# A graph network kernel: destination terms of two convolutions in SBUF by blocks of 128 rows, in place of a DMA per tile

## The reference

```python
def mesh_conv(x, src, dst, ea, w1, b1, g, bt, w2, b2):
    m = jnp.concatenate([x[dst], x[src], ea], axis=-1) @ w1 + b1
    m = jax.nn.silu(group_norm(m, g, bt))
    m = m @ w2 + b2
    out = jax.ops.segment_sum(m, dst, num_segments=n)
    ...
```

## Time and profile before

| what | value |
|---|---|
| median of 3 runs | 13,936.2 us (13,921.76 to 13,947.93) |
| span of the profiled execution | 13,635.3 us |
| its own time | not given apart from the span |
| instructions | 222,101 |
| PE matmul busy | 8536.7 us (63%) |
| DVE busy | 6628.8 us (49%) |
| POOL busy | 6588.0 us (48%) |
| ACT busy | 4239.7 us (31%) |
| convolution gathers, line 548 | 3232, 3299.7 us, mean 1021 ns |
| window matmuls, line 570 | 6464 MATMULs, 990.1 us |
| window DMAs, line 534 | 3232 of 64.0 KB |

### The profile page before, as it was taken

The page is one execution under the profiler, slowest core; times in us unless marked ns, Lnnn a source line. Parts: engine busy times, 40 slices in busy tenths (PEclk is TensorE's granted clock), DMA queues, the critical chain, the costliest instruction groups (busy, mean ns, idle before and its releaser), DMA issues. The chain is left out here.

```text
span 13635.3 us, 222101 instructions
## 1 busy us (share of the span) xinstructions
PE 8536.7 (63%) x44314; PEld 6779.2 (50%) x44314; DVE 6628.8 (49%) x13722; ACT 4239.7 (31%) x19386; POOL 6588.0 (48%) x6618
## 2 busy tenths in 40 slices
PE   3666666656566666666455556556547777777775
PEld 2444444444344444444344445445436676766664
DVE  4555555556555555555644444444453333333335
ACT  1333333333233333333222222222213333333332
POOL 4555555553455555555255555555314444444441
PEclk7777777777677777777677777777757777787776
DMA  3333333332333333333344444444334343334333
GB/s 105 87 87 89 88 88 88 88 88 69 88 87 88 87 88 89 88 87 89 90 130 130 130 131 130 129 128 129 108 77 90 88 91 89 89 89 90 88 89 88
DMA packets 1712372, 1319.86 MB, mean 97 GB/s; under 512 B 623557, under 2 KB 1489166, under 8 KB 1711480
## 3 DMA queue, kind: packets, MB, share of 16 engines
q1 hardware_dynamic: 1471910, 772.17, 20.8%
q0 software_dynamic: 237088, 539.87, 15.4%
q10 hardware_dynamic: 2610, 1.32, 0.0%
HBM read 1252.35 MB, written 60.09 MB: 96 GB/s over the span
## 5 line engine op out<-in xcount | busy, mean ns | idle before, releaser
L548 POOL DMA_INDIRECT conv_gath<-b,conv_idx x3232 | 3299.7, 1021 | 3065.9 <-DMA conv_n<-in_n_b 2120.8
L584 PE MATMUL conv_sums<-conv_hot,conv_m 128*128 128x128 f32 x6464 | 1407.6, 367 | 2188.9 <-ACT conv_m L637 1705.6
L908 POOL DMA_INDIRECT gat_gath<-g,gat_idx x1616 | 1577.6, 976 | 1956.8 <-DVE gat_val L1154 1224.5
L584 PEld LDWEIGHTS conv_sums<-conv_hot,conv_m 128*128 128x128 f32 x6464 | 1215.5, 266 | 2572.1 <-ACT acc L625 1358.5
L908 POOL DMA_INDIRECT attn_gath<-kv,attn_idx x1616 | 1583.3, 980 | 1619.0 <-DVE attn_val L1154 938.5
L672 DVE TENSOR_REDUCE conv_var<-conv_sq 128x32 f32<-128x512 f32 x808 | 550.0, 681 | 2661.3 <-ACT conv_sq L614 2335.0
L623 ACT ACTIVATE acc<-conv_sums,acc 128x1 f32 x3232 | 844.6, 261 | 2489.9 <-remote 1866.1
L570 PEld LDWEIGHTS conv_z<-conv_win,conv_hotT 128*128 128x128 f32 x6464 | 992.2, 217 | 650.4 <-issue 650.4
L939 PE MATMUL gat_p_edge<-weta,gat_xeT 128*128 128x136 f32 x3232 | 891.1, 369 | 367.8 <-ACT gat_edge L1010 280.4
L1030 ACT COPY small<-attn_smalls 40x127 f32 x1616 | 417.3, 258 | 2221.4 <-remote 1310.0
L570 PE MATMUL conv_z<-conv_win,conv_hotT 128*128 128x128 f32 x6464 | 990.1, 299 | 147.9 <-issue 134.2
(11 more groups left out here) (356 smaller groups left out, 16331.1 us busy)
## 6 DMA issues: line engine op xcount, KB each, us to landing
conv_win<-a SPq DMA_DIRECT2D x3232, 64.0 KB
conv_places<-places SPq DMA_DIRECT2D x202, 512.0 KB
attn_win<-q SPq DMA_DIRECT2D x1616, 64.0 KB
gat_xeT<-in_xeT SPq DMA_DIRECT2D x404, 256.0 KB
conv_gath<-b,conv_idx POOLq DMA_INDIRECT x3232
attn_places<-places SPq DMA_DIRECT2D x101, 512.0 KB
gat_places<-places SPq DMA_DIRECT2D x404, 128.0 KB
attn_gath<-kv,attn_idx POOLq DMA_INDIRECT x1616
```

The costliest lines, as they stand in the source:

```text
L548: pool.indirect_dma_start(gath[:, b.c * BQ + k, t, :], None, b_table, bass.IndirectOffsetOnAxis(ap=idx[:, b.c, k * QT + t:k * QT + t + 1], ...
L584: mm = nc.tensor.matmul(sums[so][:, t * P:(t + 1) * P], m[:, k, t * P:(t + 1) * P], hot[:, k, t, :], start=True, stop=True)
L908: pool.indirect_dma_start(gath[:, b.c * BQ + k, t, :], None, table, bass.IndirectOffsetOnAxis(ap=idx[:, b.c, k * QT + t:k * QT + t + 1], a ...
```

## The change

The a terms never go to DRAM. The node stage's ACT copies them into an SBUF tensor `table` of 49 blocks of 128 rows plus one block of zeros: row r of block k is in partition r. A tile's destinations span less than 128 nodes from its first one on, so they lie in the block of the first node or the next. For each tile PE multiplies two one-hots (offsets from the block's start against the partition number, and against that plus 128) with two blocks of `table`, whose address comes from a PE register. The places per tile are replaced by offsets, and a new small DMA brings 16 block bases with the metadata. The starts' DMA, SP's register load, the window DMAs and their buffers are gone. PE's step is the same order of quads and sums, cut at another point, with one load of 16 registers at the head of each batch's quads.

```diff
+            link(nc.vector.tensor_scalar(base_q[:, :], n0_q[:, :], 7, 7, ALU.logical_shift_right, ALU.logical_shift_left))
+            link(nc.vector.tensor_tensor(off_q[:, :].rearrange("q (t e) -> q t e", e=P),
+                                         dst_q[:, :].rearrange("q (t e) -> q t e", e=P),
+                                         bc(base_q[:, :].unsqueeze(2), [P, TQ, P]), ALU.subtract))
...
-            def fetch(b, nxt, _):
-                if nxt:
-                    fetch_starts(nxt)
+            def fetch(b, *_):
...
-                                 (places[:, b.c, :], places_of(D, b.i * EB, EB)),
+                                 (places[:, b.c, :], offsets_of(D, b.i * EB, EB)),
...
+                                 (bases_in[:, b.c, :], D["bases"][:, bass.ds(b.i * TB, TB)]),
...
-                _, starts = nc.values_load_multi_w_load_instructions(
-                    starts_in[0:1, b.c, :], engines=(SP_ENGINE,), min_val=0, max_val=N,
...
-                for k in range(BQ):
-                    done(sp, z_ready, b.quad(k) - WQ + 1)
-                    settle(sp, st.passed)
-                    for t in range(QT):
-                        sp.dma_start(win[:, k, t, :], a_table[bass.ds(starts[k * QT + t], P), :])\
-                          .then_inc(win_landed[k], 16)
...
+            def blocks(b):
+                pe.wait_ge(meta_landed[b.c], (b.q + 1) * META)
+                settle(pe, st.passed)
+                _, bases = nc.values_load_multi_w_load_instructions(
+                    bases_in[0:1, b.c, :], engines=(PE_ENGINE,), min_val=0, max_val=(NBLK - 1) * P,
...
-                pe.wait_ge(win_landed[s4], (b.i + 1) * QT * 16)
                 done(pe, hotT_ready, b.quad(k) + 1)
                 for t in range(QT):
-                    nc.tensor.matmul(zb[:, t * P:(t + 1) * P], hotT[:, s6, t * P:(t + 1) * P], win[:, s4, t, :],
-                                     start=False, stop=False, skip_group_check=True)
+                    for half in range(2):
+                        nc.tensor.matmul(zb[:, t * P:(t + 1) * P], hotT[:, s6, half, t * P:(t + 1) * P],
+                                         a_cols[:, bass.ds(bases[k * QT + t] + half * P, P)],
+                                         start=False, stop=False, skip_group_check=True)
...
+                if after:
+                    bases = blocks(after)
+                    pre_activation(after, 0, bases)
+                sum_up(b, 1)
+                sum_up(b, 2)
+                sum_up(b, 3)
+                if after:
+                    pre_activation(after, 1, bases)
+                    pre_activation(after, 2, bases)
+                    pre_activation(after, 3, bases)
+                if nxt:
+                    sum_up(nxt, 0)
...
-                nc.vector.tensor_scalar(hotT[:, s6, :], places[:, b.c, k * QE:(k + 1) * QE], C["iota_col"][:, 0:1], None, ALU.is_equal)\
+                nc.vector.tensor_scalar(hotT[:, s6, 0, :], places[:, b.c, k * QE:(k + 1) * QE], C["iota_col"][:, 0:1], None, ALU.is_equal)
+                nc.vector.tensor_scalar(hotT[:, s6, 1, :], places[:, b.c, k * QE:(k + 1) * QE], C["iota_col"][:, 1:2], None, ALU.is_equal)\
                   .then_inc(hotT_ready, 1)
...
-                    act.copy(made[:, :, 0:2 * P], pwb).then_inc(evacuated, 1)
+                    act.copy(table[:, bass.ds(g * GB, GB), :], pwb[:, :, 0:P])
+                    act.copy(made[:, :, 0:P], pwb[:, :, P:2 * P]).then_inc(evacuated, 1)
```

More of the change, by code:

```diff
@@ L187, in sem, with prepare @@
         return s
-def prepare(nc, w, C, D, R):
+def prepare(nc, w, C, D, R, table):
     with Stage(nc, "prep") as st:
@@ L492, in conv_edges @@
         gath_landed = [st.sem(f"gath_landed{n}") for n in range(GQ)]
-        win_landed = [st.sem(f"win_landed{n}") for n in range(WQ)]
-        starts_landed = [st.sem(f"starts_landed{c}") for c in range(RB)]
         hotT_ready, hot_ready, var_ready, normed, u_ready = (
@@ L558, in _, with pre_activation @@
             pe.wait_ge(zeroed, 2)
-            def pre_activation(b, k):
-                s6, s4, s12 = (b.c * BQ + k) % PQ, k, b.c * BQ + k
+            def blocks(b):
[3 more added lines that the diff above has]
+                    bases_in[0:1, b.c, :], engines=(PE_ENGINE,), min_val=0, max_val=(NBLK - 1) * P,
+                    skip_runtime_bounds_check_because="first nodes of blocks that hold destinations")
+                return bases
+            def pre_activation(b, k, bases):
+                s6, s12 = (b.c * BQ + k) % PQ, b.c * BQ + k
                 zb = z[s12 % ZQ]
-                pe.wait_ge(meta_landed[b.c], (b.q + 1) * META)
                 done(pe, normed, b.quad(k) - ZQ + 1)
@@ L599, in step @@
                 sum_up(b, 3)
-            for k in range(BQ):
-                pre_activation(Batch(0, 0), k)
-            pre_activation(Batch(0, 1), 0)
+                if after:
[4 more added lines that the diff above has]
+                    sum_up(nxt, 0)
+            for b in (Batch(0, 0), Batch(0, 1)):
+                bases = blocks(b)
+                for k in range(BQ):
+                    pre_activation(b, k, bases)
+            sum_up(Batch(0, 0), 0)
             run_batches(pe, step)
@@ L1314, in blocks_of, with node_stage @@
     return table[bass.ds(g * GW, GW), :].rearrange("(b p) c -> p b c", p=P)
-def node_stage(nc, kind, w, C, D, cnt, acc, acc_e, small, out, R=None):
+def node_stage(nc, kind, w, C, D, cnt, acc, acc_e, small, out, R=None, table=None):
     soft = kind in ("attn", "gat")
@@ L1363, in node_stage @@
         LOADS = 16 * {"first": 1, "conv1": 0, "conv2": 1, "attn": 3, "gat": 3}[kind]
-        STORES = 16 * {"first": 3, "conv1": 2, "conv2": 3, "attn": 4, "gat": 1}[kind]
+        STORES = 16 * {"first": 2, "conv1": 1, "conv2": 3, "attn": 4, "gat": 1}[kind]
         wide = [P, GB, P]
@@ L1823, in build @@
         cnt = sb("cnt", [P, 2, NBLK])
-        with ExitStack() as ranks:
-            def kept(name, shape, dt=F32):
-                return ranks.enter_context(nc.sbuf_tensor(f"rank_{name}", shape, dt))
-            R = {"node": kept("node", [P, NBLK]), "below": kept("below", [P, NBLK, P]),
-                 "n0_rows": kept("n0_rows", [P, NBLK, TB], I32), "dst_rows": kept("dst_rows", [P, NBLK, P], I32),
-                 "batch": kept("batch", [P, NBLK]), "batch_i": kept("batch_i", [P, NBLK], I32),
-                 "tile": kept("tile", [P, 2, NBLK + 1]), "tile_i": kept("tile_i", [P, NBLK], I32),
-                 "degree": kept("degree", [P, NBLK]), "shift": kept("shift", [P, P]), "corner": kept("corner", [P, P])}
-            prepare(nc, w, C, D, R)
-            node_stage(nc, "first", w, C, D, cnt, None, None, None, out, R)
@@ L1836, in build, with kept @@
-        with nc.sbuf_tensor("acc1", [P, NW], F32) as acc:
-            conv_edges(nc, 1, w, C, D, acc)
-            node_stage(nc, "conv1", w, C, D, cnt, acc, None, None, out)
-            conv_edges(nc, 2, w, C, D, acc)
-            node_stage(nc, "conv2", w, C, D, cnt, acc, None, None, out)
+        with nc.sbuf_tensor("table", [P, NBLK + 1, P], F32) as table:
+            with ExitStack() as ranks:
+                def kept(name, shape, dt=F32):
+                    return ranks.enter_context(nc.sbuf_tensor(f"rank_{name}", shape, dt))
+                R = {"node": kept("node", [P, NBLK]), "below": kept("below", [P, NBLK, P]),
+                     "n0_rows": kept("n0_rows", [P, NBLK, TB], I32), "dst_rows": kept("dst_rows", [P, NBLK, P], I32),
+                     "batch": kept("batch", [P, NBLK]), "batch_i": kept("batch_i", [P, NBLK], I32),
+                     "tile": kept("tile", [P, 2, NBLK + 1]), "tile_i": kept("tile_i", [P, NBLK], I32),
+                     "degree": kept("degree", [P, NBLK]), "shift": kept("shift", [P, P]), "corner": kept("corner", [P, P])}
+                prepare(nc, w, C, D, R, table)
+                node_stage(nc, "first", w, C, D, cnt, None, None, None, out, R, table)
+            with nc.sbuf_tensor("acc1", [P, NW], F32) as acc:
+                conv_edges(nc, 1, w, C, D, acc, table)
+                node_stage(nc, "conv1", w, C, D, cnt, acc, None, None, out, None, table)
+                conv_edges(nc, 2, w, C, D, acc, table)
+                node_stage(nc, "conv2", w, C, D, cnt, acc, None, None, out)
```

54 lines of the change are left out of this document (27 added, 27 removed).

## The result

| | time, us | ratio to before |
|---|---|---|
| before, median of 4 | 13,940.28 (13,921.76 to 13,947.93) | |
| after, median of 4 | 14,106.94 (14,058.73 to 14,150.32) | 1.0116 (1.0087 to 1.0144) |
| forecast | 13,235 (12,300 to 14,600) | |

The forecast had the wrong side: 167 us slower, 0.83 us for each of the 202 batches, where 707 us faster was expected. The time lies inside the range only because the range reached over to the rivals on that side. The profile of after has a span of 14,104.0 us, within 3 us of that execution's own time (14,105.77), while the one of before lies 305 us under the median of its runs. So the two profiles alone would overstate the change.

A forecast was written before the change was run, and what follows sets the result against it. No engine fills the period; a loop of waits bounds it. A batch of 21.5 + 2.5 + 3.1 = 27.1 us for 30.6 saves 707 us over 202 batches; 13,936.2 less 707 plus 6 is 13,235 us (12,300 to 14,600).

The forecast's parts named there:

- (f): In the gathers' burst: without window DMAs the stall starts only when SP issues metadata; period 27.1 us for 30.6.
- the stall: In the later half of a burst of gathers, ACT stands still for 11.76 us and SP issues DMAs slowly.
- (c): PE's 32 more MATMULs and weight loads a batch: 4.2 to 7.0 us, covered unless PE is caught in the stall.
- (a): Window DMAs, starts' load and register load leave SP's queue: 1.05 us a batch saved on average, half eaten by bases DMA.
- (b): DVE's second one-hot per quad: 2.0 us a batch, added whole, so the working stretch goes from 18.4 to 20.4 us.
- (d): PE loads 16 registers and forms 32 addresses a batch: 2.4 us at most, 0 if its sequencer runs ahead.
- PE is caught in the stall: In the convolutions, part of PE's matmuls falls behind the stall: period 33.65 us, time 14,558 us; chance 0.25.
- The variant of the first rival: In the convolutions, DVE's one-hots hold up POOL's gathers: burst 2.0 us longer, 404 us in all, time 13,639 us.
- (e): Once per kernel: one more DVE subtraction, ACT's evacuation cut in two, two table stores fewer: +6 us.
- POOL is the bound: In the convolutions, gathers follow gathers without waiting for metadata: 22.5 us a batch, time 12,300 us; chance 0.22.

The follow-up runs named there:

- a_onemm3: Changed kernel with only the first block's matmul per tile, both one-hots still made; run with the stall: 13,483.87 us, 0.9709 of before.
- a_wait2: Changed kernel plus 240 waits a batch on SP for a semaphore long set (120 more instructions in the trace); with the stall: 14,455.39 us, 1.0410 of before.
- a_min: Changed kernel with one one-hot, one matmul per tile at a constant column, no register load; without the stall: 0.9966 of before.
- a_min2: Changed kernel with one one-hot, one matmul per tile at a constant column, no register load, run again; without the stall: 0.9957 of before.
- a_rec: Changed kernel plus 240 semaphore increments a batch on SP, ahead of the next metadata; with the stall: 15,609.11 us, 1.1165 of before.
- a_static: Changed kernel with both matmuls at constant columns, no register load or address operations on PE; without the stall: 0.9920 of before, 0.9902 when run again.
- a_onehot: Changed kernel with one transposed one-hot per quad, read by both matmuls of a tile; without the stall: 0.9971 of before.
- a_onemm: Changed kernel with only the first block's matmul per tile, both one-hots still made; without the stall: 0.9991 of before.
- a_onemm2: Changed kernel with only the first block's matmul per tile, both one-hots still made, run again without the stall: 1.0004 of before.

## Why the prediction was wrong

The prediction's loop has three parts: from ACT's first copy to the first gather, the burst of 16 gathers, and from its end to the next first copy. Counted in the traces from 700 to 3000 us (means, us a batch; the parts of the forecast are those of its sum):

| | copy to first gather | burst | burst's end to copy | period |
|---|---|---|---|---|
| before | 7.3 | 21.2 | 2.1 | 30.6 |
| forecast | 3.1 | 21.5 | 2.5 | 27.1 |
| after | 6.1 | 22.2 | 3.9 | 32.3 |
| *a_onemm3* | 7.6 | 22.0 | -0.7 | 29.0 |
| *a_wait2* | 6.1 | 22.4 | 5.7 | 34.2 |

**The step that failed first is (f), the stall.** It was tied to SP's window DMAs by two coincidences in time, and the sum let ACT's copy come 14.3 us into the burst. There are no window DMAs in the burst now, and the stall stays: in the burst shown the last gather ends at 2518.82 and PE and ACT go on at one instruction per 0.71 us until 2521.4. The copy still comes behind the burst, and the 3.0 us between 6.1 and 3.1 were not saved. The trace of before had the answer in rows of PE that the prediction did not use:

```profile
2537.57 0.65 PE L584 MATMUL conv_sums<-conv_hot,conv_m 128*128 128x128 f32 x2
...
2539.41 0.36 PE L584 MATMUL conv_sums<-conv_hot,conv_m 128*128 128x128 f32 x1 [0.46 <-issue]
2541.51 0.37 PE L584 MATMUL conv_sums<-conv_hot,conv_m 128*128 128x128 f32 x1 [1.74 <-issue]
2542.20 0.37 PE L584 MATMUL conv_sums<-conv_hot,conv_m 128*128 128x128 f32 x1 [0.33 <-issue]
2543.62 1.06 PE L584 MATMUL conv_sums<-conv_hot,conv_m 128*128 128x128 f32 x2 [1.04 <-issue]
```

The eight MATMULs of one sum take 7.1 us here (2537.57 to 2544.68), where eight took 1.05 us at 2534.07, and they come 0.7, 1.4 or 2.1 us apart. SP's four DMAs in 5.01 us are the same slowing, and SP was one of its victims, not its source. ACT's wait of 11.76 us is not explained by it: the sum that it waits for was over by 2535.12, and what held back the signal is not shown. That instructions of another engine lengthen the loop is shown by *a_wait2*.

**The step that turned the sign is (c).** It priced the new matmuls at their length on PE, 4.2 us, and called them covered as long as PE isn't caught in the stall, though PE was caught in it already. They are worth 2.8 us a batch where the stall exists (*a_onemm3* against the changed kernel) and nothing, or less than nothing, where it doesn't. Without them the kernel has a gain of 416 us, 2.06 us a batch: this is what (a), (b), (d) and (f) together gave, where the sum had 3.5. So two terms were mis-sized: the gain at 2.06 for 3.5, the matmuls at 2.8 for 0; 2.8 - 2.06 is the 0.8 us a batch that was lost. Whether their number or their length on PE is the price was not separated.

**The rival "PE is caught in the stall"**, with 0.25, had the right side and the right engine, and in part the wrong mechanism. It said that the stall starts some 12 us after the first gather whatever SP does. Measured on PE, ACT and DVE it is 15.6 us before and 14.4 after, so SP's DMAs do not set it. But the 80 MATMULs did not just fit before, as the rows above show, and its price of 3.5 us a batch took the matmuls at the lower clock level: the MATMULs of line 578 take 310 ns, not 0.4 us and more, at a granted clock of 0.81 for 0.73 before. That 3.5 is near the measured 2.8 is luck. Its 14,558 us is too high because it left the gain at nothing. Its other sign, ACT's wait ending on PE's matmuls, came in part: of ACT's idle time ahead of the copies 275.5 us ended on PE and 144.4 on "remote", ahead of the square still 712.7 on "remote".

**(a)** SP's DMAs fell from 22 to 6 a batch as foretold, and the gap from the copy to the first gather by 1.2 us (7.3 to 6.1), near the 1.05 us of the sum. What that is worth by itself with the stall was not measured; without it *a_min* and *a_min2* give 31 and 46 us in all.

**(b) and the rule on the port.** The one-hot was added whole, 2.0 us. Without the stall taking it away doesn't help. The variant of the first rival, that DVE's one-hots hold up POOL by 2.0 us a batch, falls there too: the mean gather is 1043 ns with one of them and 1034 with both. With the stall the sign that I had named for it, a mean gather above 1.1 us, did come (1102 ns for 1030): the burst is 1.1 us longer (22.2 for 21.2), more than the 0.83 us that was lost, and *a_onemm3*, which makes both one-hots, keeps 22.0. *a_rec*, which makes both too, has 965 ns, but there DVE rests through most of the burst. Sorted by the DVE operation that covers over 60% of a gather, those of after (400 to 2200 us) have a mean of 944 ns with DVE idle, 1000 beside the transposed one-hots (lines 678 and 679) and 1157 beside scale and shift (lines 733 and 738). By that, an estimate, a one-hot costs some 60 ns for a gather beside it, and the larger part comes from elsewhere. No run with the stall took the one-hot out by itself, so its price there is open. By the Trainium skill, "SBUF — State Buffer", section "Who interferes with whom", a DVE operation in a two-port mode and descriptor writes exclude each other; the trace agrees that a gather takes 0.94 us alone and up to 1.3 beside DVE, but no run shows which mode the one-hot has, and without the stall taking it out shows no price.

**(d)** PE's load and addresses: without the stall *a_static* has 0.9920 and 0.9902 where the changed kernel has 0.9943 and 0.9937, so 0.2 to 0.4%, under 0.2 us a batch; covered or nearly, as said. With the stall their instructions should count; not measured. **(e)** was not tried.

**The rival "POOL is the bound"** describes the other condition: 22.5 us a batch was its figure, 21.2 to 21.5 are measured, but for the kernel before as well, so the change gains 0.6% there and not 12%. Why its gathers are 12 ns shorter (1034 for 1046) is open; of the four kernels with parts taken out only the one with all MATMULs and both one-hots keeps it (1028 and 1023 ns; the others 1038 to 1051).

**What makes the stall is not settled.** Shown: it is there in some sets and not in others for the same kernel; it comes some way into a burst of gathers and ends 2 to 3 us behind it; the engine that issues most is slowed first; instructions of an otherwise idle engine make PE issue later; the DMAs' packets take 7% longer at most. A path shared by the records and semaphore events of all engines would fit, but was not tested. The Trainium skill, "NOTIFIC — the notification-queue block", section "7.1 Overflow: three behaviours, one of which stalls the engine", says that the block inside which an engine's records are collected holds the engines back rather than lose one; *a_wait2* agrees in that more records cost more time; that the trace holds little over a third of the landings is not what the sentence says. No run here was made without recording, so whether the time would be there in an unrecorded execution is open.

## What to carry to other kernels

When several engines slow to one instruction per fixed step, count instructions beside busy time: 120 instructions that do nothing cost 2.0 us a batch here, and a matmul that "lies beside other work" is not covered. Before tying a stall to the engine seen slow in it, read the same microseconds on every other engine: the cadence of 0.7 us was on PE as well as on SP. When idle work is added to probe a limit, see that it doesn't delay its own engine's next task, as in *a_rec*. And a gain near 1% can change its sign between conditions (1.012 and 0.994 here): time the kernel before in each set, and take its profile there too.

## What was not expected of the hardware

- The same program takes 13,900 to 13,970 us or 9,731 to 9,759 us, with nothing between, by the set of runs. In the slower condition PE, ACT and SP fall to one instruction per 0.71 us in parts of a burst of gathers, and POOL, at 1.25 us a gather, does not.
- 120 instructions that only wait for a semaphore long set, on an engine that has nothing else to do, cost 2.0 us a batch there; in the other condition they cost nothing that can be measured. With 240 increments in place of them that engine became the bound: 35.1 us of its own time a batch.
- With POOL as the bound, taking work from PE and DVE made the kernel slower by 0.2 to 0.7% (*a_onehot*, *a_onemm*, *a_min* and their second runs against the changed kernel), through longer gathers. The clearest pair is in one set: 9,733.8 us for *a_onemm2* and 9,674.1 for the changed kernel, with gathers of 1048 and 1028 ns.
